# Cross-attention with a written-out loop, and part of the PSUM seeding moved from ScalarE to VectorE

## What is computed

```python
q = (layernorm(x) @ Wq)        # 16 heads of 64
k, v = ctx @ Wk, ctx @ Wv
attn = softmax(q @ k.T * 64 ** -0.5)
x = x + (attn @ v) @ Wo + bo
```

## Time and profile before

| | |
|---|---|
| median of 3 runs | 2289.66 us (2289.08 to 2293.04) |
| the profiled execution | 2283.85 us |
| its span, first to last instruction | 2281.9 us |
| mean granted TensorE clock | 0.979 |
| TensorE matmul busy | 2070.4 us, 91% |
| VectorE busy | 1498.0 us, 66% |
| ScalarE busy | 1320.5 us, 58% |
| GpSimd busy | 1430.9 us, 63% |

### The profile page before, as it was taken

One profiled execution on the slowest core, in us unless ns is written; L12 is line 12 of the kernel. 1 busy time (PEld: TensorE's weight loads), 2 busy tenths in 40 slices (PEclk: granted clock), 3 DMA queues, 4 the chain that ended last, 5 costly groups with the idle time before them and its releaser, 6 DMA issues. The chain is left out here.

```text
span 2281.9 us, 51658 instructions
## 1 busy us (share of the span) xinstructions
PE 2070.4 (91%) x19834; PEld 1532.7 (67%) x19834; DVE 1498.0 (66%) x1760; ACT 1320.5 (58%) x1593; POOL 1430.9 (63%) x652
## 2 busy tenths in 40 slices
PE   4799999999999999999999999999999778666998
PEld 3577777767777777777777767777777543225787
DVE  5666666766666667666666666666666337995685
ACT  2476767676767667666767676767676541002432
POOL 0377767766777777766777767777777722552454
PEclk9899999999999999999999999999999889997999
DMA  8010101110110112010100120101000030000320
GB/s 229 15 34 14 27 14 41 48 37 14 27 28 13 28 27 72 14 27 14 29 16 24 34 66 15 34 6 34 7 24 4 3 124 0 0 0 10 117 97 37
DMA packets 44682, 80.08 MB, mean 35 GB/s; under 512 B 7073, under 2 KB 31265, under 8 KB 43697
## 3 DMA queue, kind: packets, MB, share of 16 engines
q1 hardware_dynamic: 44464, 76.80, 11.8%
HBM read 70.03 MB, written 5.31 MB: 33 GB/s over the span
## 5 line engine op out<-in xcount | busy, mean ns | idle before, releaser
L761 POOL TENSOR_TENSOR acc<-acc,PR 128x1024 f32<-128x1024 f32 x480 | 1156.0, 2408 | 362.3 <-ACT PR L542 340.8
L617 DVE TENSOR_REDUCE amx<-ps 128x2 f32<-128x1024 f32 x512 | 626.6, 1224 | 467.2 <-PE ps L317 466.7
L542 ACT ACTIVATE PR<-ps 128x1024 f32<-128x1024 f32 x512 | 518.7, 1019 | 246.9 <-PE ps L325 246.9
L502 ACT ACTIVATE ps<-NM 128x1024 f32<-128x1024 f32 x416 | 427.1, 1028 | 200.5 <-DVE V L602 154.6
L333 PE MATMUL ps<-PR,V 128*64 128x256 f32 x4096 | 504.5, 389 | 0.1
L333 PEld LDWEIGHTS ps<-PR,V 128*64 128x64 f32 x4096 | 273.5, 138 | 162.7 <-issue 32.8
L325 PE MATMUL ps<-qh,KH 64*128 64x256 f32 x2048 | 333.4, 319 | 31.6 <-ACT ps L502 27.6
L300 PE MATMUL ps<-wv,C 64*128 64x256 f32 x4608 | 314.5, 280 | 0.6
L300 PEld LDWEIGHTS ps<-wv,C 64*128 64x128 f32 x4608 | 304.9, 187 | 10.2 <-issue 2.0
L289 PE MATMUL ps<-C,wk 64*128 64x512 f32 x2304 | 308.4, 395 | 0.8 <-DVE x L651 0.4
L325 PEld LDWEIGHTS ps<-qh,KH 64*128 64x128 f32 x2048 | 196.4, 185 | 163.0 <-issue 81.6
(11 more groups left out here) (168 smaller groups left out, 1860.3 us busy)
## 6 DMA issues: line engine op xcount, KB each, us to landing
wk<-wk_split SPq DMA_DIRECT2D x62, 192.0 KB, 3.2
wv<-wv_split SPq DMA_DIRECT2D x30, 384.0 KB, 5.0
bc<-wm_rows SPq DMA_DIRECT2D x16, 512.0 KB, 4.8
craw<-in_ctx SPq DMA_DIRECT2D x30, 256.0 KB, 3.9
we<-in_we SPq DMA_DIRECT2D x8, 768.0 KB, 6.9
wo<-in_wo SPq DMA_DIRECT2D x68, 64.0 KB, 2.1
wq<-in_wq SPq DMA_DIRECT2D x32, 128.0 KB, 2.7
craw<-in_ctx SPq DMA_DIRECT2D x30, 128.0 KB, 3.8
```

The lines of the kernel that those rows point to most:

```text
L502: act.activation(ps[:, first_bank:first_bank + 2, :].rearrange("p h (k n) -> p h k n", k=2), row.unsqueeze(2).to_broadcast([P, 2, 2, ROWS] ...
L542: act.activation(PR[:, pr_slot(t, hf), :, :, :].rearrange("p h k n -> p (h k n)"), ps[:, bank:bank + 2, :].rearrange("p h n -> p (h n)"), ...
L617: dve.tensor_reduce(amx[:, :, t, c], psG, AX.X, ALU.max).then_inc(g_max, 1)
L761: pool.tensor_tensor(flat(acc[:, :, :, :]), flat(acc[:, :, :, :]), flat(PR[:, pr_slot(t, hf), :, :, :]), ALU.add).then_inc(acc_done, 1)
```

## The change

The hardware loops are replaced by a Python loop that writes all 16 quads into the program of every engine, with all counts as constants. The seed of X for the next step's half 1, 224 of them (7 in each of 32 pairs), is written by VectorE, between the emptying of side 0 and of side 1. Those seeds and the one of half 1 at s = 0 count on a semaphore of their own, `seeded2`. The V job's wait on `v_ps` now stands before both sides. VectorE waits for its own emptying of X, for the exponential of half 0 of this step (`p_ready`) and for `NM` before it seeds.

```diff
-        def loops(eng, quad):
-            if nb > 1:
-                with eng.Fori(0, nb - 1) as b:
-                    with eng.Fori(0, NG - 1) as g:
-                        quad(b * NG + g, b, g, False, False)
-                    quad(b * NG + (NG - 1), b, NG - 1, True, False)
-            with eng.Fori(0, NG - 1) as g:
-                quad(g + (nb - 1) * NG, nb - 1, g, False, False)
-            quad(nb * NG - 1, nb - 1, NG - 1, False, True)
+        def loops(quad):
+
+            for it in range(nb * NG):
+                b, g = it // NG, it % NG
+                quad(it, b, g, g == NG - 1 and b < nb - 1, it == nb * NG - 1)
...
-                        pe.wait_ge(seeded, 2 * (it * PER + t) + hf + 1)
+                        pe.wait_ge(seeded2 if hf else seeded, it * PER + t + 1)
...
-                        seed(banks[0], row)
+                        seed(banks[0], row, seeded)
                         if has_job(t - 1, final):
                             wait_drained(act, it, t - 1, 0)
-                        seed(banks[1], row)
+                        seed(banks[1], row, seeded2)
                         weights(t, 0)
...
-                            seed(banks[1], NM[:, :, :])
+                            seed(banks[1], NM[:, :, :], seeded)
...
                     if s < NC - 1:
-                        if job is not None and s > 0:
-                            wait_drained(act, it, t, 0)
-                        act.wait_ge(p_ready, 2 * T + 1)
-                        seed(banks[0], NM[:, :, :])
                         weights(t + 1, 0)
...
-            def drain(it, job, banks):
-                for side in range(2):
+            def seed_second(first_bank, pair, T):
+
+                dve.wait_ge(p_ready, 2 * T + 1)
+                dve.wait_ge(nm_sb, pair + 1)
+                dve.tensor_copy(ps[:, first_bank:first_bank + 2, :].rearrange("p h (k n) -> p h k n", k=2),
+                                NM[:, :, :].unsqueeze(2).to_broadcast([P, 2, 2, ROWS])).then_inc(seeded2, 1)
+
+            def drain(it, job, banks, sides):
+                for side in sides:
...
-                        if side == 0:
-                            dve.wait_ge(v_ps, v_num(it, job) + 1)
+                        dve.wait_ge(v_ps, v_num(it, job) + 1)
...
                     if has_job(t, final):
-                        drain(it, JOBS[t], [low_bank(t), psB])
+                        drain(it, JOBS[t], [low_bank(t), psB], (0,))
+                    if s < NC - 1:
+                        if has_job(t, final):
+                            wait_drained(dve, it, t, 0)
+                        seed_second(score_bank(t, 0), p, T)
+                    if has_job(t, final):
+                        drain(it, JOBS[t], [low_bank(t), psB], (1,))
```

More of the change, by code:

```diff
@@ L102, in cross_attention @@
         g_ps, g_max = sem("g_ps"), sem("g_max")
-        seeded, seeded_h1, s_ps, p_ready, pv_done = sem("seeded"), sem("seeded_h1"), sem("s_ps"), sem("p_ready"), sem("pv_done")
+        seeded, seeded2, seeded_h1, s_ps, p_ready, pv_done = sem("seeded"), sem("seeded2"), sem("seeded_h1"), sem("s_ps"), sem("p_ready"), sem("pv_done")
         acc_done, fold_done = sem("acc_done"), sem("fold_done")
@@ L267, in quad @@
                 load_wo(of_next(1), 1)
-            loops(sp, quad)
+            loops(quad)
         @block.tensor
@@ L466, in quad @@
                         row_sums(False)
-            loops(pe, quad)
+            loops(quad)
             pe.wait_ge(wo_in[0], (nb * NG + 1) * 32)
@@ L498, in max_diagonals, with seed @@
                 ins.then_inc(m_diag, 1)
-            def seed(first_bank, row):
+            def seed(first_bank, row, done):
                 act.activation(ps[:, first_bank:first_bank + 2, :].rearrange("p h (k n) -> p h k n", k=2),
-                               row.unsqueeze(2).to_broadcast([P, 2, 2, ROWS]), ACT.Copy).then_inc(seeded, 1)
+                               row.unsqueeze(2).to_broadcast([P, 2, 2, ROWS]), ACT.Copy).then_inc(done, 1)
             act.wait_ge(craw_in[0], 64)
@@ L585, in quad @@
                         context_hi(j, craw[:, :, :])
-            loops(act, quad)
+            loops(quad)
         @block.vector
@@ L672, in _ @@
                     dve.wait_ge(wv_in, 128)
-                drain(0, job, [ps[:, 2 * (i % 2), :], ps[:, 6 if i % 2 == 0 else 3, :]])
+                drain(0, job, [ps[:, 2 * (i % 2), :], ps[:, 6 if i % 2 == 0 else 3, :]], (0, 1))
                 if i in (1, 4):
@@ L694, in quad @@
                             split_q(1 - pi, p + 1)
-                        dve.wait_ge(seeded, 2 * T + 2)
+                        dve.wait_ge(seeded2, T + 1)
                         dve.tensor_copy(NM[:, :, :].rearrange("p h n -> p (h n)"), psN).then_inc(nm_sb, 1)
@@ L721, in quad @@
                         context_lo(j, craw[:, :, :])
-            loops(dve, quad)
+            loops(quad)
             dve.wait_ge(pv_done, PAIRS * NC + 2)
@@ L765, in quad @@
                         pool.tensor_tensor(accf[:, :, :], acc[:, :, 0, :], acc[:, :, 1, :], ALU.add).then_inc(fold_done, 1)
-            loops(pool, quad)
+            loops(quad)
 def norm_sems(sem, name):
```

## The result

The changed kernel took 2328.22 us (median of 4 runs, 2322.34 to 2331.22) against 2289.37 us for the kernel before (4 runs): ratio **1.0172**, 95% interval 1.0137 to 1.0207. It is slower, by almost exactly the amount forecast. The experiments show that both terms of this total, the loop's gain and the seed's cost, were forecast too small, and that inside the seed's cost the plain quads were forecast too large.

What follows compares the result with a forecast made beforehand. It took TensorE, 96.5% busy in the attention part, as the bound. Seed losses of 59.2 us (52.2 + 1.25 + 5.7) less 20.6 won by the written-out loop gave +38.6, from 2289.66 to 2328 us; range 2293 to 2352.

Steps and rivals of the forecast that it cites:

- What bounds the kernel, and that ScalarE's relief is worth nothing to TensorE: Attention part: TensorE, 96.5% busy, is the bound; taking 230 us of seeds off ScalarE gains nothing.
- The seed's length: VectorE's new 1024-column copy takes 1.23 us, bounds 1.03 and 1.39, and starts 0.04 behind the emptying.
- the rival of a copy at ScalarE's 1.03 us: VectorE writes the seed as fast as ScalarE, loss and gain cancel: 2294 us, chance 0.06.
- Two-round steps: Steps t = 3, 4, 5, 11, 12, 13: scores wait 0.17 to 0.26 us for the seed, 1.34 per quad.
- Three-round steps: Steps t = 1, 2, 6, 9, 10, 14: late third reduction delays the next guess, 0.49 us in t = 1, 2.14 per quad.
- The sign named for it: TensorE's idle time before the guesses (L317, waiting for reductions at L617) rises by 30 us.
- Steps 0 and 8 free: Steps without reductions lose nothing: seed 0.4 us early in t = 0, just in time in t = 8.
- Batch ends: Three quads where VectorE also splits the next context lose 1.9 us net each, bounds 0 and 4, 5.7 in all.
- For the registers that go I give nothing: Constant counts in place of loop registers gain nothing, as the last quad has the same stops inside it.
- The jumps: Loop jumps pause TensorE: eight inner ones 2.14 us each, outer ones 3.04 + 0.38; written out gives back 20.6.
- the rival that it stays: The pause at a quad's start belongs to VectorE's divide chain and remains: 2349 us, chance 0.05.
- The rival of a short copy: The copy runs at two columns per cycle, 0.69 us, so the seed is hidden: 2269 us, faster, chance 0.16.

Runs made afterwards that it cites:

- e1: Kernel before with only the loop written out, all seeds left on ScalarE: 2258.55 us, 0.9877 of the kernel before.
- e9: e1 with GpSimd's two adds of each pair's last step left out, so the row sums miss a chunk: 2240.85 us, 0.9786 of the kernel before.
- e4: Changed kernel, but VectorE seeds only in the two-round steps s = 3, 4, 5, ScalarE in the others: 2283.61 us, 0.9986 of the kernel before.
- e6: Changed kernel with VectorE's third reduction put ahead of the second half of the emptying: 2311.54 us, 1.0126 of the kernel before.
- e8: Changed kernel, but ScalarE seeds everything in the three quads at a batch's end: 2292.37 us, 1.0036 of the kernel before.
- e11: Changed kernel without GpSimd's adds in the three batch-end quads, all but each pair's first: 2312.53 us, 1.0118 of the kernel before.
- e2: Kernel before with only the seed moved to VectorE, hardware loops kept: 2388.05 us, 1.0451 of the kernel before.
- e10: e2 with two of the three waits between emptying and seed moved ahead of the emptying: 2354.25 us, 1.0278 of the kernel before.
- e3: Changed kernel, but VectorE seeds only the second of the two banks and ScalarE the first: 2261.80 us, 0.9905 of the kernel before.
- e5: Changed kernel, but VectorE seeds only in the three-round steps s = 1, 2, 6, ScalarE in the others: 2296.13 us, 1.0043 of the kernel before.
- e7: e3 with ScalarE seeding both banks in the three quads at a batch's end: 2243.22 us, 0.9810 of the kernel before.

## Why the prediction was right, and where it was not

The forecast was 2328, measured 2328.22. That the two agree within a microsecond is chance: four runs of the changed kernel lie between 2322 and 2331. The two terms of its sum, from the row-max matmuls of the profiles of before, e1 and changed:

| term, us | forecast | by pairs | by ratios |
|---|---|---|---|
| loop written out | -20.6 | -24.9 | -28 |
| of it at batch ends, with the pair behind | -3.4 | -9.7 | |
| seed on VectorE | +59.2 | +63.3 | +68 |
| of it 12 plain quads | +41.8 | +34.6 | |
| of it 3 batch-end quads | +16.1 | +28.2 | +31 |
| of it the last quad | +1.3 | +0.5 | |
| sum | +38.6 | +38.4 | +39 |

- *What bounds the kernel, and that ScalarE's relief is worth nothing to TensorE*: right for the chain as argued. Wrong as "worth nothing": it brought GpSimd's adds forward and took the collision with the division away. In e1 TensorE waits for the division 23 times in the plain quads, 10.3 us in all, and in the changed kernel not at all there (e9 shows the cause). So the 34.6 us of the plain quads are net: the late steps cost about 45, 3 more than the 41.8 forecast, and 10 came back.
- *The seed's length*: 1.23 forecast from L700 and a reduction, 1228 ns measured. The wait behind the emptying 0.04, measured 0.03 to 0.04 in written-out code. Right; with it the rival of a copy at ScalarE's 1.03 us is out.
- *Two-round steps*: 0.24 forecast in t = 4, 0.25 in the row. e4 confirms the sum of the three steps in each pair. Right.
- *Three-round steps*: 0.49 in t = 1; measured 3.72 against 3.32 from emptying to guess is 0.40, and from the scores' start to the guess it is 0.48 more than before. e6 shows that it is the guess, and that the projection would be next. Right to a tenth. The sign named for it, 30 us more idle before the guesses, was wrong: it is 19, because part of the lateness is hidden behind modelled ends of matmuls.
- *Steps 0 and 8 free*: not quite. In t = 8 the scores come 0.2 us late (TensorE idle 0.18 before them for the seed); "just in time" was too tight.
- *Batch ends*: the step that was mis-sized most: "I take 1.9 net" on top of a plain quad, measured 9.4 less 2.9, so 6.5. e8 shows the size. That those quads have no slack on VectorE and that every late end of a split delays the load behind it is argued and not shown; that splits meet GpSimd is shown, and e11 says what it costs the pairs there: 5.7 us in one place, 0.3 in each of the two others.
- *For the registers that go I give nothing*: true of TensorE's steps in the kernel before, as e1's first pairs show. It was luck for the seed: I worked out its cost as if in written-out code, from L625 and L627, whose wait in the kernel before has only one count behind it. In loops it costs 0.17 us more (e2, e10). My expectation for e2, 2349, was wrong by 39 us, for this reason above all.
- *The jumps*: the pause is theirs (e1), the rival that it stays is out. Its size was nearly right in the middle of a batch (15.2 us by pairs where 17.2 were forecast), too small at the ends.
- *The rival of a short copy*: e3, which halves the copy, lands near where that rival was priced, 2269 forecast, 2262 measured. Its mechanism was right in the plain quads, where the loss is gone; only the copy's length was not the fast one. Its total fits partly by luck: the batch ends still lose 17.7 us, which it had at nothing, and the division and the loop give back what it did not count.

So the total was met by luck: the batch ends cost 12 us more than forecast, and against that the plain quads cost 7 less and the loop gave 4 more. Nothing in the argument vouched for that.

What stays open: why the batch ends gain 9.7 us from the written-out loop, and how much of the 28 us there is VectorE's own work and how much the loads that start later.

The ratios go by all runs, the pairs by one execution of each kernel, and they differ by up to some 10 us. Behind the last row-max matmul the changed kernel's profiled execution is 7 us longer than that of the kernel before (498.2 against 491.0), with a mean granted clock of 0.77 against 0.86 in the 60 us behind it:

```profile
1790.00:1850.00 60.00, 41.01 (x335) 27.30 (x337) 9.69 (x11) 32.40 (x35) 41.25 (x19) 0.86 0.01 3
```

```profile
1829.00:1889.00 60.00, 43.26 (x323) 28.19 (x323) 14.28 (x16) 25.17 (x26) 36.95 (x18) 0.77 0.01 3
```

(Busy time by stretch, before and changed, columns as in the earlier trace rows.) Most of the 7 us is in the attention's last pair, and the change is not their cause. From the last row-max matmul to the last weighted sum it is 52.6 to 52.7 us in the three executions with a mean granted clock of 0.90 there (e3, e8, e11), 55.8 to 55.9 with 0.85 (before, e2, e4), 57.3 to 57.5 with 0.82 (e1, e5, e9) and 60.4 with 0.77 (changed, e6, e7, e10). The changed kernel and e11 have the same code there, and so have e1 and the kernel before, whose last quad is written out already. What sets the clock in one execution or another stays open.

## What to carry to other kernels

An engine that is 65% busy has no 35% to give: what counts is the slack between its chain and the next matmul at each step, here 0.03 us behind the seed in one kind of step and 0.77 behind the third reduction in the other. Work that takes another engine's place fits if it is longer by less than that slack, and work that is added to a chain if it is shorter than it. Half the seed fitted in both and cost nothing in the plain quads; the whole one cost 63 us in all. Price the stretches with the least slack (here the batch ends) by themselves, and look at what the third engine does once the second is relieved. In a hardware loop, keep waits on computed counts ahead of the instruction before, not between two links of the chain.

## What the runs showed of the hardware

- Two waits on counts held in registers, between two VectorE instructions, put 0.17 us more between them (0.20 against 0.03), in loops only; moved ahead of the first instruction they cost nothing there.
- A VectorE instruction with both inputs in SBUF stood still while GpSimd added: 0.42 us became up to 2.40, 1.75 became up to 3.83, and a GpSimd add of 2.4 us became 3.57 behind it.
- A jump back in a hardware loop cost TensorE a pause of 1.7 to 2.5 us, and straight code none.
- The same code took 52.7 us at a mean granted TensorE clock of 0.90 (the attention's last pair in e11) and 60.4 us at 0.77 (in the changed kernel).
- VectorE's copy from SBUF into PSUM took 695 ns for 512 columns and 1228 for 1024; the same copy on ScalarE 602 and 1028.
